# Second attention of a two-layer transformer kernel: scores made twice in place of turned probabilities

## The reference

```python
scores = jnp.einsum('bhqd,bhkd->bhqk', q, k_h) / math.sqrt(HEAD_DIM)
causal = jnp.triu(jnp.ones((t, t), dtype=bool), k=1)
scores = jnp.where(causal[None, None], jnp.finfo(scores.dtype).min, scores)
attn = jax.nn.softmax(scores, axis=-1)
ctx = jnp.einsum('bhqk,bhkd->bhqd', attn, v_h)
ctx = ctx.transpose(0, 2, 1, 3).reshape(b, t, D_OUT)
return ctx @ Wo
```

## Time and profile before

| | |
|---|---|
| time, median of 3 runs (1176.55 to 1178.55) | 1177.67 us |
| span of the profiled execution | 1175.2 us |
| busy PE, DVE, ACT, POOL | 1135.8, 780.6, 705.3, 410.5 us |
| granted clock of PE, mean | 0.999 of full |

### The profile page before, as it was taken

The page is one execution under the profiler, slowest core; times in us unless marked ns, Lnnn a source line. Parts: engine busy times, 40 slices in busy tenths (PEclk is TensorE's granted clock), DMA queues, the critical chain, the costliest instruction groups (busy, mean ns, idle before and its releaser), DMA issues. The chain is left out here.

```text
span 1175.2 us, 20479 instructions
## 1 busy us (share of the span) xinstructions
PE 1135.8 (97%) x6634; PEld 952.6 (81%) x6634; DVE 780.6 (66%) x2463; ACT 705.3 (60%) x1646; POOL 410.5 (35%) x342
## 2 busy tenths in 40 slices
PE   7899999999999999999999999999999899999997
PEld 6788888788888888888888778888888677777786
DVE  6866776667776667766677762223336899999775
ACT  6656665556665566666566544543112899999524
POOL 4654554255444445534443513334013210020200
PEclk9999999999999999999999999999999999999999
DMA  6011110111110100110100012222001223321001
GB/s 230 19 40 43 37 32 24 30 28 37 53 29 21 37 32 24 55 27 11 45 19 28 1 37 75 68 78 76 1 18 24 57 70 80 98 53 33 2 1 72
DMA packets 30364, 51.24 MB, mean 44 GB/s; under 512 B 5680, under 2 KB 6576, under 8 KB 30256
## 3 DMA queue, kind: packets, MB, share of 16 engines
q1 hardware_dynamic: 29680, 48.85, 14.7%
q10 hardware_dynamic: 576, 1.05, 0.2%
HBM read 38.35 MB, written 2.10 MB: 34 GB/s over the span
## 5 line engine op out<-in xcount | busy, mean ns | idle before, releaser
L487 POOL TENSOR_TENSOR turned<-turned,sin 128x512 f32<-128x512 f32 x73 | 94.4, 1293 | 310.3 <-ACT turned L347 310.3
L363 ACT ACTIVATE probs<-probs,neg_max 128x256 f32<-128x256 f32 (+1 forms) x256 | 119.8, 473 | 11.3 <-DVE neg_max L580 11.3
L1477 ACT ACTIVATE a_probs<-a_probs,a_neg_max 128x512 f32<-128x512 f32 (+3 forms) x256 | 122.6, 562 | 0.1
L1661 DVE CUSTOM_DVE_ANT_0 a_probs<-bank,a_mask 128x512 f32<-128x512 f32 (+3 forms) x256 | 109.8, 486 | 6.2 <-PE bank L1881 6.1
L490 POOL TENSOR_TENSOR turned<-turned,by_cos 128x512 f32<-128x512 f32 x73 | 101.1, 1385 | 5.7
L96 PE MATMUL bank<-wo_hi,oT_hi 128*128 128x512 f32 x256 | 100.3, 392 | 1.7 <-DVE oT_lo L643 1.7
L734 PE MATMUL bank<-xT_hi,wq_hi 128*128 128x512 f32 x256 | 101.7, 397 | 0.0
L734 PE MATMUL bank<-xT_lo,wq_hi 128*128 128x512 f32 x256 | 100.3, 392 | 0.0
L734 PE MATMUL bank<-xT_hi,wq_lo 128*128 128x512 f32 x256 | 100.0, 391 | 0.0
L96 PE MATMUL bank<-wo_hi,oT_lo 128*128 128x512 f32 x256 | 99.9, 390 | 0.0
L96 PE MATMUL bank<-wo_lo,oT_hi 128*128 128x512 f32 x256 | 99.7, 389 | 0.0
(11 more groups left out here) (234 smaller groups left out, 3155.1 us busy)
## 6 DMA issues: line engine op xcount, KB each, us to landing
staged<-weights SPq DMA_DIRECT2D x70, 256.0 KB, 2.7
f_staged<-weights_f SPq DMA_DIRECT2D x33, 256.0 KB, 2.7
a_q_stack<-a_qT_hi SPq DMA_DIRECT2D x64, 64.0 KB, 2.0
rows<-x_rows SPq DMA_DIRECT2D x2, 1024.0 KB, 7.4
a_k_stack<-a_kT_hi SPq DMA_DIRECT2D x64, 32.0 KB, 2.0
a_q_stack<-a_qT_lo SPq DMA_DIRECT2D x32, 64.0 KB, 2.0
out<-rows SPq DMA_DIRECT2D x8, 256.0 KB, 2.0
a_raw<-weights_qkv SPq DMA_DIRECT2D x4, 384.0 KB, 4.4
```

Source lines behind the costliest of these rows:

```text
L363: act.activation(probs[:, s % 2, h, 0:width], probs[:, s % 2, h, 0:width], ACT.Exp, bias=neg_max[:, s % 2, h:h + 1], scale=SCALE0, accum_o ...
L487: pool.tensor_tensor(at, at, sin[:, :], ALU.mult).then_inc(sin_done, 1)
L1477: act.activation(row_probs(s, qt), row_probs(s, qt), ACT.Exp, bias=neg_max[:, h, qt:qt + 1], scale=-1.0).then_inc(exp_done, 1)
L1661: dve.tensor_tensor_reduce(row_probs(s, qt), ps_s[bank][:, at:at + seen], mask[:, SEQ - seen:SEQ], -SCALE1, HIGHEST, ALU.add, ALU.min, neg ...
```

## The change

The probabilities are no longer turned. The scores are still made with queries on partitions, but only for their row maxima: DVE writes the masked scores to a place that nobody reads, and the negated maxima of two heads to eight columns of `row_maxima`. PE turns that tile (`turn_maxima`), ACT copies the eight rows and, on its own DMA queue, sends them to rows 96 and 97 of `q_stack`, where `k_stack` has rows of ones (`send_maxima`). Then PE makes the scores again with operands exchanged (`shifted_scores`), keys on partitions and over 97 or 98 rows, so the maxima are already subtracted. ACT takes the exp straight from the three banks into the ring (now 8 heads), POOL sets what lies above the diagonal to zero with two selects a head (`causal`), and `apply` waits for that. The evacuation goes from DVE to ACT. There are four stack buffers in place of two, each cleared and given its ones by POOL at the start. First scores run 5 slots ahead. At the end the turned outputs stand in the last slots, and the last value products between the first two tiles of the output projection.

```diff
-RING = 6
+RING, RING_OVER_X = 8, 6
+STACKS = 4
...
-AHEAD_SCORES, AHEAD_MAXIMA, AHEAD_EXPS = 3, 2, 1
+AHEAD_SCORES = 5
+HEAD_PAIRS = SLOTS1 // 2
...
+        def maxima_sent(s):
+            return (s + AHEAD_SCORES - 2) // 2
+
+        def maxima_bank(n):
+            return ps_t[0] if n < 2 else ps_o[(n // 2 - 1) % 2]
...
+            for u in range(UNITS1):
                 if u == KV1:
                     sp.wait_ge(part_lo, TURNS_OF[1])
-                sp.wait_ge(scored, PIECES * GROUP1 * (u - 1))
+                if u < STACKS:
+                    sp.wait_ge(stacks_set, 4 * (u // 2 + 1))
+                else:
+                    sp.wait_ge(shifted_ready, PIECES * GROUP1 * (u - STACKS + 1))
                 load_stacks(u)
...
             def exps(s):
-                h = s % GROUP1
-                for qt in ROW_TILES:
-                    act.wait_ge(max_done, SEQ_TILES * s + maxima_before(qt))
-                    act.activation(row_probs(s, qt), row_probs(s, qt), ACT.Exp, bias=neg_max[:, h, qt:qt + 1],
-                                   scale=-1.0).then_inc(exp_done, 1)
-
-            def copy_turned(s):
                 if s >= RING:
                     act.wait_ge(applied, 2 * ((s - RING) // GROUP1 + 1))
-                for piece in (1, 2):
+                for piece in range(PIECES):
                     width, at = TURNED_WIDTH[piece], piece * SEQ
-                    act.wait_ge(pT_ready, PIECES * s + piece + 1)
-                    act.activation(pT[:, s % RING, at:at + width], ps_t[piece][:, 0:width], ACT.Copy).then_inc(pT_act, 1)
+                    act.wait_ge(shifted_ready, PIECES * s + piece + 1)
+                    act.activation(head_probs(s)[:, at:at + width], ps_t[piece][:, 0:width], ACT.Exp,
+                                   scale=SCALE1).then_inc(exp_done, 1)
+
+            def send_maxima(n):
+
+                u, pair = divmod(n, 2)
+                act.wait_ge(max_turned, n + 1)
+                if n >= 4:
+                    act.wait_ge(max_in[n % 4], 16 * (n // 4))
+                act.activation(turned_maxima[0:2 * SEQ_TILES, n % 4, :], maxima_bank(n)[0:2 * SEQ_TILES, 0:P],
+                               ACT.Copy).then_inc(max_copied, 1)
+                act.wait_ge(max_copied, n + 1)
+                act.dma_start(q_stack(u)[STACK:STACK + 2, pair, :].bitcast(F32),
+                              turned_maxima[0:2 * SEQ_TILES, n % 4, :].bitcast(F32)).then_inc(max_in[n % 4], 16)
+
+            def evacuate(n):
+                act.wait_ge(applied, 2 * (n + 1))
+                if n >= 1:
+                    act.wait_ge(o_turned, n)
+                act.activation(oT_now[:, :], ps_o[n % 2][:, :], ACT.Copy).then_inc(o_read, 1)
...
+            send_maxima(0)
+            send_maxima(1)
+
+            def high_out(tile):
+                act.wait_ge(out_turned, tile + 1)
+                act.activation(outT_hi[:, :, tile * P:(tile + 1) * P], out_bank(tile), ACT.Copy).then_inc(out_hi, 1)
+
+            for s in range(SLOTS1):
+                exps(s)
                 if s == 0:
                     copy_values(TILES - 1)
                     act.wait_ge(v_done, TILES)
+                if s % 2 == 1 and maxima_sent(s) < HEAD_PAIRS:
+                    send_maxima(maxima_sent(s))
                 if s in PARTS_IN_LOOP:
                     high_part(PARTS_IN_LOOP[s])
-
-            def high_out(tile):
-                act.wait_ge(out_turned, tile + 1)
-                act.activation(outT_hi[:, :, tile * P:(tile + 1) * P], out_bank(tile), ACT.Copy).then_inc(out_hi, 1)
+                if s % GROUP1 == 2 and s >= GROUP1:
+                    evacuate(s // GROUP1 - 1)
+                if s >= SLOTS1 - 3:
+                    high_out(s - SLOTS1 + 3)
...
-            pool.memset(k_stack[:, :, :, :].bitcast(F32), 0.0).then_inc(pads_set, 1)
+            pool.memset(row_maxima[:, :, :], 0.0).then_inc(pads_set, 1)
             pool.memset(v_flat[:, :], 1.0).then_inc(pads_set, 1)
+            for n, stacks in enumerate(k_stacks):
+                pool.memset(stacks[:, :, :, :].bitcast(F32), 0.0).then_inc(stacks_set, 1)
+                pool.wait_ge(stacks_set, 4 * n + 1)
+                pool.memset(stacks[STACK:STACK + 1, :, 0, :].bitcast(F32), 1.0).then_inc(stacks_set, 1)
+                pool.memset(stacks[STACK:STACK + 2, :, 1, :].bitcast(F32), 1.0).then_inc(stacks_set, 1)
+                pool.wait_ge(stacks_set, 4 * n + 3)
+                pool.memset(stacks[STACK:STACK + 1, :, 1, :].bitcast(F32), 0.0).then_inc(stacks_set, 1)
+                pool.wait_ge(stacks_set, 4 * n + 4)
...
+            def causal(s):
+
+                pool.wait_ge(exp_done, PIECES * (s + 1))
+                for at, step in DIAGONALS:
+                    blocks = head_probs(s)[:, at:at + 2 * step].rearrange("p (a c) -> p a c", a=2)[:, :, 0:P]
+                    masked = pool.affine_select(out=blocks, in_=blocks, pattern=[[0, 2], [1, P]], base=0, channel_multiplier=-1,
+                                                compare_op=ALU.is_ge, fill=0.0)
+                masked.then_inc(causal_done, 1)
+
             turn_rows(TILES - 1)
-            for s in range(2, SLOTS1):
-                pool.wait_ge(pT_dve, s)
+            for s in range(SLOTS1):
+                causal(s)
...
-                if s >= GROUP1:
-                    dve.wait_ge(pT_ready, PIECES * (s - GROUP1 + 1))
+                n = s // 2
+                if n >= 4:
+                    dve.wait_ge(max_turned, n - 3)
                 for qt in ROW_TILES:
                     bank, at = SCORES_AT[qt]
                     seen = (qt + 1) * P
+                    to = s % 2 * SEQ_TILES + qt
                     dve.wait_ge(scored, PIECES * s + bank + 1)
-                    dve.tensor_tensor_reduce(row_probs(s, qt), ps_s[bank][:, at:at + seen], mask[:, SEQ - seen:SEQ],
-                                             -SCALE1, HIGHEST, ALU.add, ALU.min,
-                                             neg_max[:, s % GROUP1, qt:qt + 1]).then_inc(max_done, 1)
-
-            def copy_turned(s):
-                if s >= RING:
-                    dve.wait_ge(applied, 2 * ((s - RING) // GROUP1 + 1))
-                dve.wait_ge(pT_ready, PIECES * s + 1)
-                dve.tensor_copy(pT[:, s % RING, 0:SEQ], ps_t[0][:, :]).then_inc(pT_dve, 1)
-
-            def evacuate(n):
-                dve.wait_ge(applied, 2 * (n + 1))
-                if n >= 1:
-                    dve.wait_ge(o_turned, n)
-                dve.tensor_copy(oT_now[:, :], ps_o[n % 2][:, :]).then_inc(o_read, 1)
+                    dve.tensor_tensor_reduce(unread(s, qt), ps_s[bank][:, at:at + seen], mask[:, SEQ - seen:SEQ],
+                                             -1.0, HIGHEST, ALU.add, ALU.min,
+                                             row_maxima[:, n % 4, to:to + 1]).then_inc(max_done, 1)
...
+            for s in range(AHEAD_SCORES):
+                maxima(s)
+            rotate(TILES - 1)
+            for s in range(SLOTS1):
+                if s + AHEAD_SCORES < SLOTS1:
+                    maxima(s + AHEAD_SCORES)
+                if s in PARTS_IN_LOOP:
+                    low_part(PARTS_IN_LOOP[s])
+                if s % GROUP1 == 3 and s >= GROUP1:
+                    join(s // GROUP1 - 1)
+                if s >= SLOTS1 - 3:
+                    low_out(s - SLOTS1 + 3)
...
-            def turn(s):
-
-                pe.wait_ge(exp_done, SEQ_TILES * (s + 1))
+            def turn_maxima(n):
+
+                u = n // 2
+                pe.wait_ge(max_done, SEQ_TILES * (2 * n + 2))
+                if n >= 1:
+                    pe.wait_ge(max_copied, n)
+                if n == 2:
+                    pe.wait_ge(v_done, TILES)
+                    pe.wait_ge(sin_done, 4 * TILES)
+                if n == 4:
+                    pe.wait_ge(part_lo, len(TURNS))
+                if u >= 3 and n % 2 == 0:
+                    pe.wait_ge(finished, u - 2)
+                pe.transpose(maxima_bank(n)[:, 0:P], row_maxima[:, n % 4, :], ident[:, :]).then_inc(max_turned, 1)
+
+            def shifted_scores(s):
+
+                u, h = divmod(s, GROUP1)
+                n = s // 2
+                if s == 0:
+                    pe.wait_ge(stacks_set, 8)
+                    pe.wait_ge(max_copied, 2)
+                if h % 2 == 0:
+                    pe.wait_ge(max_in[n % 4], 16 * (n // 4 + 1))
+                rows_in = STACK + 1 + h % 2
                 for piece, tiles in enumerate(((0,), (1, 3), (2,))):
                     if s >= 1:
-                        if piece == 0:
-                            pe.wait_ge(pT_dve, s)
-                        else:
-                            pe.wait_ge(pT_act, 2 * (s - 1) + piece)
+                        pe.wait_ge(exp_done, PIECES * (s - 1) + piece + 1)
                     for kb in tiles:
-                        for qt in range(kb, SEQ_TILES):
-                            at = TURNED_AT[kb][1] + (qt - kb) * P
```

(39 more changed lines are left out.)

154 lines of the change are left out of this document (62 added, 92 removed).

## The result

| | before | after |
|---|---|---|
| time, median of 4 runs each | 1177.16 us | 1164.68 us (1163.67 to 1166.21) |
| ratio, 95% interval | | 0.9893 (0.9879 to 0.9907) |
| span of the profiled execution | 1175.2 us | 1161.8 us |
| one clean unit of the loop | 11.03 us | 9.75 us |

The kernel is faster, by 12.5 us. The forecast was 1143.5, 34 us under the kernel before, with a range to 1160, which does not hold the result. The sign came out right, the likeliest case did not.

A forecast was written before the change was run, and what follows sets the result against it. PE was to bind the changed loop at 8.8 us per unit. Terms 2.9 - 0.9 - 31.2 - 0.5 - 4.5 = -34.2 on the 1175.2 us span gave 1141.0; the median lies 2.5 higher, 1143.5 us, range 1136 to 1160.

The forecast's parts named there:

- (c): Loop, slots 4 to 60: 14 units at 8.8 us instead of 154.4 us in all, minus 31.2 us.
- the gain of slot 59: End of the loop: slot 59 has no score left to make, minus 0.5 us.
- rival 2: Loop: uneven slots and one-deep buffers make a unit 9.5 to 9.9 us, 1153 to 1159 us; chance 0.2.
- (a): Start: GpSimd's longer first fills delay PE's first rotated rows once, plus 2.9 us.
- (b): From the loop's first PE work to slot 4: 15.3 us instead of 16.2, minus 0.9 us.
- (d): Slot 60 to the output projection, last value product included: 10.9 us instead of 15.4, minus 4.5 us.
- (e): Everything outside the other stretches: left as it is, forecast difference 0.
- 3 (the maxima's way round): Loop: ACT's copy, DMA and semaphore for the maxima end last; at landings of 4.0 us, 1160 us; chance 0.1.
- 4 (selects bind): Loop: GpSimd's selects bind from 1.1 us each; at 1.6 us each, 1206 us; chance 0.06.

The follow-up runs named there:

- experiment 1: Changed kernel with the four output turns of every fourth slot ahead of that slot's scores instead of behind them: 1166.87 us.
- experiment 2: Changed kernel with the transfers of the turned maxima issued by GpSimd instead of ACT, the copy staying on ACT: 1164.76 us.
- experiment 3: Changed kernel with both output turns ahead of the scores and the maxima's transfers issued by GpSimd: 1158.87 us.
- experiment 11: Changed kernel with value products in three parts, earlier output turns, start, weight-request and tail edits, large last loads split, maxima sent by GpSimd: 1143.40 us.
- Experiment 5: Changed kernel with GpSimd filling the second pair of stacks after tile 6's rotated rows, not before tile 0's: 1162.33 us.
- Experiment 12: The kernel of experiment 11 plus 23 useless transposes in PE's pauses ahead of the first shifted scores: 1142.21 us.
- Experiment 7: Changed kernel with slot 4's scores waiting for half a stack only, and ACT splitting the last weights ahead of the last output's copy: 1167.27 us.
- experiment 9: Changed kernel, old slots, with earlier output turns, GpSimd sending maxima, start, weight-request and tail edits, and the output's division one slot later: 1148.00 us.

## Why the prediction was wrong

**The step that failed is (c), with "So PE binds, with 0.2 lost": 8.8 us a unit.** PE's work was 8.6, as forecast (the shifted scores cost some 0.2 more than the 0.70 a slot, the rest as much less). The waits were 1.15 a unit against my 0.2: 14 x 0.95 = 13.3 us. The 0.2 stood for the exponentials behind a sending, which cost 0.5; the wait for DVE, 0.65, I had put at nothing. With the stall in unit 3 (1.4), the longer unit from slot 4 (10.09 instead of 9.75, 0.3) and the gain of slot 59, of which little came (0.2 of 0.5), that makes the 15.3 us between -31.7 and -16.4. I had added up each engine's load over a unit and compared sums. The mechanism was before me as rival 2, at a chance of 0.2, and its 9.5 to 9.9 a unit holds the measured 9.75. What spoke against it, "pieces let an engine run a slot ahead", is refuted: a score bank is free only once its maxima are taken, so in two slots without a value product PE and DVE go in step, and ACT's in-order queue takes the sending ahead of the exponentials. That the two chains end together is shown by experiments 1 to 3 (0.00, 0.30 and together 0.63 us). That nothing else of size binds is seen in experiment 11, where 0.1 us of waits is left in a unit.

**(a), +2.9, measured +3.95.** The wait was right (idle 3.09 us, PE 2.5 later at its rotated rows). Missing was the clock behind the wait, 1.2 us in the next products, and 0.3 in the turn itself (0.69 instead of 0.43). Experiment 5 shows it.

**(b), -0.9, measured +0.35.** The second stack was waited for as forecast: 920.77 is 4.5 behind the mark, forecast 4.3, and the shifted scores began 6.04 behind it, forecast 5.7. The sign failed in the next four slots, 10.5 us instead of 9.6, at half the clock. The windows view of 922 to 928 us, before and after:

```profile
922.00:928.00 6.00, 3.87 (x23) 2.79 (x22) 5.05 (x20) 5.27 (x14) 1.13 (x2) 1.00 0.20 46
```

```profile
922.00:928.00 6.00, 5.65 (x20) 5.19 (x21) 5.61 (x27) 4.52 (x10) 3.14 (x6) 0.50 0.36 85
```

My sum took all durations at the clock of 1.00 of the earlier trace rows and did not ask what the new pauses ahead of the loop do to it. Experiment 12 shows, in the best version, that these pauses are the cause there; for the changed kernel this is inferred.

**(d), -4.5, measured -3.75.** 11.7 us instead of 10.9; no run takes this stretch apart.

**(e), "The rest I leave as it is", measured +2.5.** The output's copy that went to ACT has its last instance at the head of ACT's tail, where it waits for the last value product, with the weights' split, a table load and the root of tile 0 behind it. Experiment 7 gives 2.2 of the 2.5 back.

**Not in the sum at all: the output weights.** The diff moves their request from unit 3 to unit 5. I read the four stack buffers as a gain for SP and did not ask what else hangs on SP's loop. In the changed kernel it cost 1.4 us, but up to 7.3 in the versions of the experiments, part of it by the clock behind the wait.

**The rivals.** 3 (the maxima's way round) does not occur in the changed kernel, where PE never waits for that transfer in the loop; 2.0 us of landing were enough. It occurs in unit 7 of experiments 2, 3 and 9, which send by GpSimd beside 1 MB of other loads. 4 (selects bind) is excluded: two take 0.77 us a slot and GpSimd is busy 42% of the time. The Trainium skill's per-element model for it ("GPSIMD Engine Reference", section 3.1) gave 0.4 to 0.55 us as an estimate; the trace agrees with its lower end, 406 ns. The range, which ended where rivals 2 and 3 did, failed because rival 2 was priced with forecast edges: at 9.75 a unit it gives 1143.5 + 13.3 = 1156.8, and the misses of (a), (b), (d) and (e), 1.05, 1.25, 0.75 and 2.5, with unit 3's 1.4, add 7.0, together 1163.8.

## What to carry to other kernels

Before adding up engine loads, write one period slot by slot with the buffers' depth: where two groups that share one buffer stand closer than the other engine's time for it, that slot is as long as that engine's, and spare time elsewhere in the period does not pay it back. When a forecast says that an instruction costs little on an engine with spare time, ask what stands behind it in that engine's queue: 0.62 us of issue on an engine busy 66% of the time cost 0.3 to 0.4 us of every unit (experiments 2 and 11). When a loop gets more buffers, look at all that the feeding queue's loop issues, since requests placed by its index move with it.

## What the runs showed of the hardware

Behind a wait of PE of 3.1 us the granted clock fell from the higher level (0.50 to 0.75 on the mean from 885 to 890 us), which added 1.2 to 2.5 us to 24 products in every one of eight kernels, and in none of those without the wait. Behind five gaps of 0.4 to 0.8 us in PE's weight loads (from 913 to 917 us in experiment 11) it was at the lower level for 6 us, and filling them with useless work took that away. Behind a wait in the middle of the loop, with GpSimd's wait at 3.1 to 3.6 us, the clock was 0.86 on the mean of slots 12 to 16 in three kernels and stayed at 1.00 in one with 3.6 and one with 3.9.

The issue of a 4 KB transfer kept ACT for 0.62 us, and GpSimd for 0.56. A fill of 1024 columns on one or two partitions takes GpSimd 0.95 us (one of the six took 1.11), about half of the 1.81 us for 2048 columns on all 128: thin fills cost by their columns, as I had assumed.

One transfer of maxima took 4.8 us from its issue to PE's first use, where 2.0 is the median landing, beside 1 MB of loads from another engine's queue.
